# GpSimd's factors for the first norm moved into the odd group, and the seven early tiles' row loads sent ahead

## What is computed

```python
# block 1: graph layer, x is (8, 1024, 128), adj is (8, 1024, 1024)
h = layernorm(x)                                     # "first norm"
agg = eps * h + einsum('bnm,bmd->bnd', adj, h)
h = silu(rmsnorm(agg @ W1 + b1) * rms_w)             # hidden 512
x = x + h @ W2 + b2
# block 2: mixture of 8 experts, the best 2 of each token
z = layernorm(x)                                     # "second norm"
combine = softmax over the top 2 of (z @ Wg.T + bg), scattered to (.., 8)
for e in range(8):
    y = relu(z @ F1[e].T + fb1[e]) @ F2[e].T + fb2[e]
    out += combine[..., e:e+1] * y
x = x + out
```

## Time and profile before

| | us |
|---|---|
| median of three runs | 649.16 |
| the three runs | 642.61, 649.37, 649.16 |
| the profiled execution, its own time | 644.73 |
| its span in the trace | 643.0 |
| its mean granted TensorE clock | 0.991 of full speed |

### The profile page before, as it was taken

One profiled execution on the slowest core, in us unless ns is written; L12 is line 12 of the kernel. 1 busy time (PEld: TensorE's weight loads), 2 busy tenths in 40 slices (PEclk: granted clock), 3 DMA queues, 4 the chain that ended last, 5 costly groups with the idle time before them and its releaser, 6 DMA issues.

```text
span 643.0 us, 14755 instructions
## 1 busy us (share of the span) xinstructions
PE 588.4 (92%) x4379; PEld 540.5 (84%) x4379; DVE 425.8 (66%) x1255; ACT 368.2 (57%) x932; POOL 439.1 (68%) x728
## 2 busy tenths in 40 slices
PE   1799999999999999999999789999999999999972
PEld 0678888788887888879888689999999999999940
DVE  2557979889798898888877754444444544444454
ACT  4367487575865757657667544554555455455411
POOL 4232387968869698696886787667667667767650
PEclk9989999999999999999999989999999999999998
DMA  7952343144422443234541577767766766777698
GB/s 259 397 179 96 131 160 110 64 162 165 157 71 102 166 160 143 58 133 165 154 133 69 195 253 249 262 236 250 258 248 243 260 247 239 257 251 246 230 396 362
DMA packets 42614, 127.29 MB, mean 198 GB/s; under 512 B 8155, under 2 KB 20872, under 8 KB 40488
## 3 DMA queue, kind: packets, MB, share of 16 engines
q1 hardware_dynamic: 33320, 108.88, 46.9%
q0 software_dynamic: 8640, 16.93, 7.8%
q10 hardware_dynamic: 576, 0.53, 0.3%
HBM read 61.19 MB, written 24.02 MB: 133 GB/s over the span
## 4 chain that ended last, share of the span: by engine, by line
PE 58%; POOL 15%; ACT 6%; DVE 6%; issue 6%; DMA 5%; SPq 3%; POOLq 0%; DVEq 0%; ACTq 0%
PE ps_g L752 9%; PE ps_y L752 8%; POOL slots L1042 7%; PE ps_agg L526 5%; PE ps_y L586 5%; PE ps_agg L528 4%; PE ps_agg L527 4%; PE ps_t L533 4%; PE ps_h L526 4%; PE ps_h L528 4%; PE ps_h L527 4%; POOL x_all L1035 3%; PE ps_t L731 2%; DMA expert_w<-parts 2%; DMA adj_in<-slots 2%
## 5 line engine op out<-in xcount | busy, mean ns | idle before, releaser
L1113 POOL DMA_INDIRECT parts<-adj_in x142 | 139.5, 982 | 71.2 <-ACT adj_in L947 55.4
L1042 POOL DMA_INDIRECT slots<-rows,dest x128 | 127.5, 996 | 22.9 <-issue 22.6
L947 ACT ACTIVATE adj_in<-adj_in,share 128x128 f32<-128x128 f32 x142 | 49.4, 395 | 116.9 <-issue 106.6
L805 ACT ACTIVATE adjT_hi<-ps_t 128x512 fp32r<-128x512 f32 x128 | 76.0, 595 | 59.9 <-PE ps_t L533 59.9
L1155 DVE TENSOR_TENSOR adjT_lo<-ps_t,adjT_hi 128x512 fp32r<-128x512 f32 x128 | 87.5, 688 | 29.2 <-ACT adjT_hi L805 26.6
L533 PEld LDWEIGHTS ps_t<-ident,adj_in 128*128 128x128 f32 x512 | 77.9, 191 | 24.7 <-issue 13.4
L533 PE MATMUL ps_t<-ident,adj_in 128*128 128x128 f32 x512 | 79.0, 278 | 13.1 <-POOL adj_in L1014 13.1
L1411 DVE TENSOR_TENSOR adjT_lo<-ps_t,adjT_hi 128x256 fp32r<-128x256 f32 x71 | 30.1, 425 | 73.8 <-ACT adjT_hi L929 73.8
L526 PE MATMUL ps_agg<-adjT_hi,xn_split 128*128 128x512 f32 (+1 forms) x162 | 71.0, 438 | 7.8 <-DVE adjT_lo L1155 7.7
L752 PE MATMUL ps_y<-W2e,hb 128*128 x576 | 70.8, 276 | 0.0
L752 PEld LDWEIGHTS ps_y<-W2e,hb 128*128 128x128 f32 x576 | 68.1, 193 | 0.2 <-issue 0.2
(11 more groups left out here) (239 smaller groups left out, 1404.5 us busy)
## 6 DMA issues: line engine op xcount, KB each, us to landing
adj_in<-in_adj SPq DMA_DIRECT2D x16, 2048.0 KB, 8.9
wcur<-expert_w SPq DMA_DIRECT2D x54, 578.0 KB
xn_split<-expert_w SPq DMA_DIRECT2D x17, 578.0 KB
adj_in<-slots SPq DMA_DIRECT2D x71, 130.0 KB
expert_w<-parts SPq DMA_DIRECT2D x8, 512.0 KB, 10.0
out<-x_all SPq DMA_DIRECT2D x8, 512.0 KB, 7.0
x_all<-in_x SPq DMA_DIRECT2D x1, 3072.0 KB, 19.5
parts<-adj_in POOLq DMA_INDIRECT x142
```

The source lines that it names most:

```text
L805: act.activation(adjT_hi[m % 2][:, :], ps_t[m % 2][:, :], ACT.Copy).then_inc(s_hi, 1)
L947: ins = act.activation(ye[ku][:, j, :], yb[ku % 2][:, j, :], ACT.Copy, scale=share[ku][:, j:j + 1])
L1042: pool.indirect_dma_start(out=slots, out_offset=bass.IndirectOffsetOnAxis(ap=dest[q % 2][:, c, j:j + 1], axis=0), in_=rows[q % 2][:, c, j, ...
L1113: pool.indirect_dma_start(out=parts, out_offset=bass.IndirectOffsetOnAxis(ap=goes[u % 8][:, j, :], axis=0), in_=ye[ku][:, j, :], in_offset ...
```

## The change

Two things are changed. In GpSimd's program `ln1_factors` for graph b+1 no longer stands at the end of the even group but in the odd group that follows, behind `ln2_factors` and `rms_factors` and ahead of `add_eps`. In SyncE's program the early tiles are loaded in another order, and their row loads wait for less.

```diff
             def load_rows(t, k, rows_):
-                wait(sp, s_eT, t - 3)
-                wait(sp, s_ysc[k], added(t // 4 - 1))
-                wait(sp, s_share, t - 3)
+                if isinstance(t, int) and t < EARLY:
+                    wait(sp, s_slot[k], 16 * (t // 4))
+                else:
+                    wait(sp, s_eT, t - 3)
+                    wait(sp, s_ysc[k], added(t // 4 - 1))
+                if not isinstance(t, int) or t >= EARLY:
+                    wait(sp, s_share, t - 3)
...
-            for t in range(4):
+            for t in range(2):
                 load_rows(t, t, of_table(t)[0])
             sp.wait_ge(s_wTa, 2 * E)
             sp.wait_ge(s_wTd, E)
             sp.wait_ge(s_fb1c, 1)
             sp.wait_ge(s_fb2, 16)
-            for t in range(4):
+            for t in range(2):
                 load_weights(t, t, of_table(t)[1])
+            for t in range(2, 4):
+                load_rows(t, t, of_table(t)[0])
+            for t in range(2, 4):
+                load_weights(t, t, of_table(t)[1])
+            for t in range(4, EARLY):
+                load_rows(t, t % 4, of_table(t)[0])
             sp.wait_ge(s_tail, 1)
...
                 if t >= 4:
                     rows_, expert = of_table(t)
-                    load_rows(t, k, rows_)
+                    if t >= EARLY:
+                        load_rows(t, k, rows_)
                     load_weights(t, k, expert)
...
                 if has(g, 1):
                     rms_factors(g - 1)
+                if par == 1 and has(g, -1):
+                    pool.wait_ge(s_mv1, b + 2)
+                    ln1_factors()
                 if has(g, -1):
                     add_eps(g + 1, 1 - par, b + par)
...
-                if par == 0 and has(g, -2):
-                    pool.wait_ge(s_mv1, b + 2)
-                    ln1_factors()
```

## The result

| | before | after |
|---|---|---|
| median, us | 647.5 | 641.66 |
| runs | 642.6 to 649.5 (20 runs) | 637.2 to 645.7 (20 runs) |
| the profiled execution's own time, us | 644.73 | 640.99 |
| its span, us | 643.0 | 639.2 |
| mean granted clock | 0.991 | 0.990 |

The ratio of the times is 0.9919, with a 95% interval of 0.9899 to 0.9939: 0.8% faster, 5.2 us (the two medians of the table lie 5.8 us apart). The prediction was 640.5 us, with 635 to 648 as its range and "within 1%" as the likeliest class, and both hold.

What follows compares the result with a forecast made beforehand. TensorE, busy 588.4 of 643.0 us, was taken as the bound, so only its idle stretches could give time. 2.3 + 3.65 = 5.95, so 6.0 us: 638.7 from the profile, 643.2 from the median; forecast 640.5, range 635 to 648.

Steps and rivals of the forecast that it cites:

- within 1%: Class for the whole kernel's time against before: chance 0.54, beside faster by over 1% 0.38 and slower 0.08.
- Part one: Odd groups: GpSimd starts the second norm's factors sooner, ending TensorE's wait for normed rows; 2.3 us, between 0 and 2.9.
- ScalarE's 208.1: Odd group: the moved first norm's factors are ready at 208.0 to 208.1, 0.3 us late for ScalarE, mostly covered.
- the price of one stall: Odd groups: each TensorE wait for normed rows removed gains 0.58 us, five times, at most 2.9 us.
- The 0.6 us I took off for short waits of ScalarE: Deduction from 2.9 us for ScalarE's short waits, also in groups 1 and 3, leaving 2.3 us.
- Part two: Seam between the kernel's two parts: SyncE's new load order gains 3.05 + 0.60 = 3.65 us.
- Tile 7's term: Seam: fill landed by 383, scatter in 2 to 4 us, so TensorE's 0.60 us wait for tile 7's rows goes.
- 3.05 us for tiles 0 to 4: Seam: tile 4's first layer runs at 380.0 instead of 383.05, a 2.4 us weights wait replacing the 2.97 us rows wait.
- A late scatter: Rival at the seam: the last scatter delays tile 7's rows, capping the gain at 2.8 us; chance 0.10.
- The 2.97 us for tile 4's rows: Seam: TensorE's longest wait in the profile before, expected to go once these rows are loaded ahead of the fills.
- The lead: Tiles after the seam to tile 70: TensorE is the bound and a lead of a few us stays to the end.
- Clock: Seam: the new 2.4 us wait brings no lower clock, as the 1.90 us wait brought none; otherwise 1.7 us goes.

Runs made afterwards that it cites:

- GpSimd's half: Kernel before with only GpSimd's move of `ln1_factors`, SyncE's order as before: 641.62 us, ratio 0.9926.
- thin cover: Kernel before with GpSimd's move of `ln1_factors` plus six rests ahead of the odd groups' scatters, SyncE's order as before: 647.04 us, ratio 1.0004.
- SyncE's half: Kernel before with only SyncE's new load order and the row loads' changed waits, GpSimd's program as before: 647.49 us, ratio 1.0004.
- weights first: Changed kernel without the early row loads of tiles 4 to 6; weights of tiles 0 and 1 still go right behind their rows: 641.93 us, ratio 0.9918.
- rows ahead: Changed kernel with tiles 0 to 3 loaded in the old order, but rows 4 to 6 still ahead of the fills: 641.68 us, ratio 0.9919.
- the two on the slower chips: Kernel before, unchanged, run twice more on chips where it took longer: 714.46 and 705.69 us.

## Why the prediction was right, and where it was not

The spans of the seven traces on the comparable chips, cut in five: to the first transposes of hidden rows in group 2; from there to tile 0's transposes; to tile 8's; to the last tile's; to the end. The first three have SyncE's old order at the seam, the others the new one or a half of it.

| kernel | start | first part | seam | tiles 8 to 70 | end |
|---|---|---|---|---|---|
| before | 66.83 | 295.66 | 31.49 | 213.22 | 35.80 |
| GpSimd's half | 67.15 | 291.22 | 29.73 | 213.10 | 35.90 |
| thin cover | 70.56 | 296.48 | 32.02 | 213.04 | 35.60 |
| after | 67.58 | 292.56 | 28.90 | 214.41 | 35.75 |
| SyncE's half | 70.20 | 295.71 | 28.90 | 213.78 | 35.51 |
| weights first | 70.20 | 291.17 | 28.76 | 213.55 | 36.32 |
| rows ahead | 70.73 | 291.26 | 28.92 | 213.06 | 36.23 |

**Part one: right in mechanism, too small by half.** GpSimd's start, VectorE's and TensorE's waits, ScalarE's 208.1 and the idle time ahead of the even group came as worked out. The step that failed is the price of one stall. I took TensorE's idle time, 0.58 us, as what a stall costs. But the idle time is counted from the modelled end of the matmuls in front. Before, L557 began 1.19 us after the start of the transposes ahead of it; after, 0.44 us, as the two then overlap. That is 0.75. Then the next matmul, which began 0.59 us after L557's start, begins 0.46 after, for another 0.13:

```profile
204.55 0.61 PE L544 MATMUL ps_t<-ident,adj_in 128*128 128x128 f32 x4
204.99 0.60 PE L568 MATMUL ps_y<-ident,rows 128*128 128x128 f32 x4
205.45 0.50 PE L537 MATMUL ps_agg<-adjT_hi,xn_split 128*128 128x512 f32 x1
```

Together 0.88, which is just what the group became shorter by. (205.49 in the earlier trace rows is the same L557 of before.) Five times 0.88 is 4.4 us, the 4.4 of the table, and 4.8 us (3.0 to 6.5) by the times. The Trainium skill (Perfetto Trace Analysis, the TensorE part of the lifecycle) says that a matmul's end in the profile is computed, not observed; this trace agrees. Starts can be set against each other, idle times only from below. The 0.6 us I took off for short waits of ScalarE was for nothing: no such wait reached TensorE.

**Part two: the long wait went, the gain did not come.** Three steps failed here.

*Tile 7's term.* Of the two terms, 3.05 us for tiles 0 to 4 and 0.60 for tile 7, the first came out against the trace that it was priced on: tile 4's first layer ran 20.56 us behind tile 0's transposes (383.05, 362.49) and now runs 17.68 behind (377.82, 360.14), 2.9 us sooner. The second failed. I had the last fill landed by 383, 20.5 us behind tile 0's transposes, and the last scatter in 2 to 4 us, so that tile 7's rows are in time. The fill landed 23.1 us behind in after, 22.8 with weights first and 23.0 with rows ahead, as ScalarE issued it only 18.3 to 19.9 us behind and it took 3.1 to 4.8 us. The scatter took 5.5 us in after, 5.99 in SyncE's half and 3.8 with weights first. So tile 7's rows wait for whichever of the two lands last, the fill in three kernels and the scatter in one, and TensorE waits 0.17 to 1.23 us for them. In the three traces of the old order the fill came last too.

Tile 7 thus becomes the gate of the seam: 28.9, 28.9, 28.8 and 28.9 us in four kernels whose waits ahead of it are quite different, and whose mean granted clocks from tile 0 to tile 8 are too (1.00, 1.00, 0.94 and 0.88). No run moved the fill or the scatter on the comparable chips, so this is read from the traces and not tested. A late scatter was in my rivals, at 0.10, with a cap of 2.8 us for the seam; 2.6 us came, against the trace of before. A late fill was in none.

*The price, taken from one trace.* The 2.97 us for tile 4's rows is not there in any other trace of the old order: none in GpSimd's half, 0.55 us with the thin cover, and none of 0.3 us or more in the two on the slower chips. By the table the old order's seam takes 29.73 to 32.02 us, 31.1 on average, so the gain at tile 8 is 2.2 us by traces, not 3.65.

*The lead.* I wrote that a lead of a few us stays to the end. It does not show there.

**What became of these 2.2 us** is settled only in part, and it was not seen in the times. The stretch from tile 8 to the last tile takes 213.7 us on average with the new order and 213.1 with the old one. In three of the four new ones the last tile's rows come 1.2 to 1.6 us late: SyncE's loads of the landed counts stand just ahead of them, and an earlier TensorE may only wait longer there, which no comparable run tested. The end adds 0.2. So the traces leave 1.4 us, on three and four executions, and the times give −0.3 with 1.2 at the upper end of the interval. The parts ahead of the seam differ more than that from execution to execution: the start takes either about 67 or about 70.5 us, with either order. It goes with the clock there: the granted mean from 26 to 42 us is 0.89 in the three short starts and 0.68 to 0.79 in the four long ones. I can't say more than that SyncE's half is worth something between a loss of 1.7 and a gain of 1.2 us by the times, and not the 3.65 that I gave it.

**Clock.** No lower clock followed the 1.11 us wait at the seam of after, as I took it. In the trace with the thin cover 2.11 us for tile 7's rows were followed by it (0.53 and 0.50 in the second and third microsecond behind), and the seam of GpSimd's half, with 1.78 us for its first weights, has a mean of 0.89:

```profile
358.40:388.10 29.70, 25.82 (x202) 25.19 (x203) 17.63 (x63) 12.71 (x40) 26.06 (x45) 0.89 0.83 283
```

So the wait of 1.90 us that was not followed by it, on which I leaned, proves little.

**The sum.** 2.3 + 3.65 was 5.95; it is 4.8 + 0.4, the rest of the whole change's 5.2, and 0.4 is not told from nothing. Two errors of 2.5 and 3.3 us lay on opposite sides, so the number was right by luck.

## What to carry to other kernels

Price a stall by the distance between the starts of the instructions around it, with and without the wait, not by the idle time in front of one. Before a wait is priced, look for it in a second trace of the same kernel. When a wait ahead of a gate goes, list everything that the gate itself waits for (here the landing of a scatter and of a fill, neither in the queue whose order was changed) and take each landing from rows measured under the most similar load. And when a helper's work is moved under cover, measure what is left of the cover: here 0.93 us, and 1.4 us beyond it the same stall was back in the next group.

## What the chip showed that I had not expected

The eps additions of GpSimd now run beside VectorE's small gate operations. Two of these take 0.49 and 0.44 us instead of 0.19 each:

```profile
209.06 0.49 DVE L1182 TENSOR_TENSOR tied<-score,top 128x32 f32<-128x32 f32 x1
209.58 0.44 DVE L1184 TENSOR_TENSOR tied<-tied,falling 128x32 f32<-128x32 f32 x1
```

The pair at L1212 (L1201 of before) that the additions lay beside before took 1.44 us and now takes 0.87. The group became shorter by 0.88 us, all of it accounted for at L557, so the slower gate cost nothing that shows. The Trainium skill (SBUF — State Buffer, two separate sides) says that the ports shared by VectorE and GpSimd are an exclusive lock against which the loser fully blocks, and that a VectorE operation with two SBUF inputs is one that needs it. Two such operations stretched by 0.3 us beside additions of 0.5 us each agree with that, and so does the reduction between 208.84 and 209.03, which has one input and kept its 0.19 us beside the same additions.

Three row loads of 130 KB took SyncE 3.71 us to issue at 364.18, 1.0 to 1.2 us each, against 1.90 us for four, 0.33 us each, with no weights ahead of them: behind four weight loads their issue was dearer. The three weight loads from 373.56 on, 4.01 us together against 2.24, are no such case: each was issued in 0.49 to 0.53 us, and 2.2 us of the stretch SyncE waited for tile 2's result before the third.
